# Closing stages of a two-layer graph attention by pairs of node tiles

## The chip, the cores and the metric

The kernel is one program on one core of a Trainium2 chip. The metric is the device time of a whole launch in microseconds (us), as the median of several runs.

## The reference, cut to what matters

12500 nodes of 256 features, padded to 98 tiles of 128 nodes; 200000 edges, sorted by destination. First comes a node network with a residual, then two layers of graph attention, four heads of 64 and one head of 256.

```python
x = x + L0_gnn(relu(layernorm(x)), ...)       # segment sums, MLP 608 -> 1024 -> 256
h = relu(layernorm(x))
def gat(h, W, a_src, a_dst, b, heads):
    h = (h @ W).reshape(n, heads, -1)
    al_s, al_d = sum(h * a_src), sum(h * a_dst)        # per node and head
    e = leaky_relu(al_s[src] + al_d[dst], 0.2)         # every node has an edge to itself, too
    m = segment_max(e, dst); ex = exp(e - m[dst])
    den = segment_sum(ex, dst)
    return segment_sum(h[src] * (ex / den[dst]), dst) + b
h = elu(gat(h, W1, ..., b1, heads=4))
x = x + gat(h, W2, ..., b2, heads=1)
```

## The kernel before, in words

The program runs stage after stage. A stage (`stage`, line 44) has its own buffers and semaphores and ends in a barrier of all engines, so that nothing of one stage runs beside another. Every engine has its own program within a stage and they meet in semaphores. `steps` (line 905 and after) writes the first and last turns of a loop out and puts the others into a hardware loop; `At` gives the index `n`, a buffer `slot` and a `par`ity.

1. `structure`, `masks` and `edge_chains`: tables of the edges, and sums and maxima along them. The change leaves these alone.
2. `node_mlp`: 49 steps, each with a pair of node tiles. TensorE multiplies; VectorE adds the first products (`add_first`, line 1564), makes features and statistics and turns PSUM into SBUF; ScalarE has ReLU and square roots; GpSimd gathers rows. The result `x1` of the node network goes to DRAM, and so does `table1`, which is the layer-normed `x1` times the weights of the first attention, with its scores of sources (`als`) behind it; the scores of destinations (`ald`) stay in SBUF. In a step TensorE waits for the hidden rows of this pair (`hid_ready`, line 1450) before it makes the table rows of the pair before (line 1456).
3. `clear`: GpSimd (line 1899) and VectorE (line 1904) write zeros to the accumulators `acc`, 98 tiles of 264 numbers per partition.
4. For each of the two layers: `open_layer` splits `ald` into three bf16 numbers (lines 1637 to 1641, VectorE alone), `attention` walks over 64 batches of 26 groups of edges, and `close_layer` makes rows of nodes of the sums.
5. `attention`: GpSimd gathers 26 times per batch (line 578) by the indices that SP has loaded (line 530); TensorE, ScalarE and VectorE make weights and add the products to `acc`. VectorE first clears `drow` (line 906), and SP's loads (lines 522 to 536) begin behind the wait for it (`blank`).
6. `close_layer` (lines 1651 to 1865) has a lead and a loop over 98 node tiles. In the lead the weights and the bias are loaded, VectorE projects the attention vectors of the second layer through its weights (first layer only, lines 1266 and 1267), and then works out the share of the sums, `ga`, and that of the node's own edge, `gb`, for all nodes (lines 1812 to 1828), with two exponentials on ScalarE. The loop, first layer, with what an engine does for one tile `n`:
   - SP loads the node's own row (`hrow`, four buffers, line 1705) and stores the table row of tile `n-2` (line 1719).
   - GpSimd: `own = hrow * gb` (line 1736), then `own + bias` (line 1741).
   - VectorE: `t1 = acc * ga` (line 1846), `y = t1 + own` (line 1849), `mn = min(y, 0)` (line 1852), and for tile `n-1` the last of the ELU, `h2 = exp(mn) - 1 + relu(y)` (line 1862).
   - ScalarE: ReLU, exponential, the zeros for `acc` of this tile (lines 1779 to 1781); then, for `n-2`, it copies the projection out of PSUM (`als`, `ald`, `grow`, lines 1789 and 1791); then, for `n-1`, the turned rows to SBUF (line 1795).
   - TensorE, for `n-1`: two transposes of `h2` (line 1756), a wait until ScalarE has copied them, then two multiplications by the second layer's weights (line 1763; each has two records in the trace).

   In the last layer there are no TensorE and ScalarE parts in the loop. `x1` is loaded too (`xrow`, line 1707), `t1 = acc * ga + xrow` is one instruction (line 1843), GpSimd and `y` are as above, and `y` is stored as the output (line 1715).

## Time and profile before

| | us |
|---|---|
| median of three runs | 6883.79 (6879.75 to 6888.57) |
| the profiled execution, its own time | 6892.58 |
| its span, first to last instruction | 6890.8 |
| TensorE busy | 4795.7 (70%) |
| VectorE busy | 4425.4 (64%) |
| GpSimd busy | 3704.5 (54%) |
| ScalarE busy | 3018.8 (44%) |
| mean granted TensorE clock | 0.836 of full |

No engine is busy all the time. As the stages follow one another behind barriers, the span is a sum of stages, and shares of the whole span say little: each stage is to be read by itself. The last column but one of a windows row is the granted clock: 1.00 is 2.4 GHz and 0.50 is 1.2 GHz.

### The profile page before, as it was taken

To read this page: it belongs to the slowest core of one execution; us is meant where nothing else is said; L and a number is where in the kernel's file an instruction comes from. 1 tells how busy PE (TensorE), PEld (TensorE's weight loads), DVE (VectorE), ACT (ScalarE), POOL (GpSimd) and SP (SyncE) were. 2 spreads that over 40 slices of the span, in tenths; PEclk is the share of its full clock that TensorE was granted. 3 is DMA by queue.
4 is the path that set the end of the run, shared out by engine and by line. 5 is a ranking of instruction groups with operands and counts; after the bars stand their busy time and mean duration, and the time that the engine had idled before them with its cause. 6 is when DMAs were issued, how large, how long until landed. Compare 5 with 4: busy or idle time off the path is not lost. (4 is left out here: it accounts for less than half of the span.)

```text
span 6890.8 us, 105434 instructions
## 1 busy us (share of the span) xinstructions
PE 4795.7 (70%) x22853; PEld 3495.8 (51%) x22853; DVE 4425.4 (64%) x12670; ACT 3018.8 (44%) x8326; POOL 3704.5 (54%) x4025
## 2 busy tenths in 40 slices
PE   0065666999995777777777776757777777777770
PEld 0044445777773555555555554535555555555540
DVE  7399996555554666666666666645555555555558
ACT  4044442222223666666666665534433443443330
POOL 5200000111106777777777774457777777777758
PEclk9988888999996888888888887558888888888885
DMA  1299996333323444444444443334444444444437
GB/s 37 85 371 396 402 400 231 105 104 104 105 96 91 119 119 121 120 119 119 121 119 120 121 119 75 83 87 109 110 109 109 110 109 110 109 110 110 109 85 220
DMA packets 382596, 964.82 MB, mean 140 GB/s; under 512 B 105887, under 2 KB 222982, under 8 KB 357399
## 3 DMA queue, kind: packets, MB, share of 16 engines
q0 software_dynamic: 168928, 459.50, 25.4%
q1 hardware_dynamic: 206504, 452.76, 19.2%
q10 hardware_dynamic: 7056, 51.38, 1.9%
q8 instruction: 35, 0.57, 0.0%
q14 instruction: 73, 0.60, 0.0%
HBM read 696.58 MB, written 266.77 MB: 140 GB/s over the span
## 5 line engine op out<-in xcount | busy, mean ns | idle before, releaser
L578 POOL DMA_INDIRECT rows<-table_d,idx x3328 | 3160.3, 950 | 1048.0 <-issue 899.4
L639 PE MATMUL pG<-rows,onehot 128*128 128x264 f32 (+1 forms) x6656 | 2175.9, 474 | 585.6 <-issue 343.8
L639 PEld LDWEIGHTS pG<-rows,onehot 128*128 128x128 f32 x6656 | 1487.4, 236 | 1119.9 <-issue 462.1
L866 DVE TENSOR_TENSOR acc<-acc,pG 128x264 f32 (+1 forms) x3328 | 1417.7, 426 | 966.9 <-PE pG L639 587.6
L730 ACT ACTIVATE rows<-rows 128x64 f32<-128x64 f32 (+1 forms) x4480 | 1249.9, 368 | 0.0
L723 ACT ACTIVATE onehotT<-pQ 128x1024 bf16<-128x1024 f32 (+1 forms) x512 | 442.4, 864 | 1317.8 <-PE pQ L611 1317.8
L712 ACT ACTIVATE onehot<-pQ 128x1024 f32<-128x1024 f32 (+1 forms) x512 | 441.1, 862 | 536.3 <-PE pQ L596 533.5
L1152 PE MATMUL pH<-hT_pre,w1h 128*128 128x256 f32 x1568 | 437.9, 436 | 212.3 <-ACT pre L1090 204.3
L1210 DVE SCALAR_TENSOR_TENSOR run<-run,same_e,ea 128x96 f32<-128x96 f32 x1567 | 490.1, 313 | 4.9 <-DMA ea<-in_ea 4.2
L1210 DVE SCALAR_TENSOR_TENSOR run<-run,cut_e,ea 128x96 f32<-128x96 f32 x1567 | 490.0, 313 | 0.1
L1152 PEld LDWEIGHTS pH<-hT_pre,w1h 128*128 128x128 f32 x1568 | 333.4, 221 | 297.3 <-ACT pre L1090 222.8
L848 DVE TENSOR_TENSOR rows<-rows,pA 128x1024 f32<-128x1024 f32 x384 | 466.8, 1216 | 4.4
L1393 POOL COPY idx_agg<-k_end 128x2 int32 (+1 forms) x49 | 9.0, 184 | 748.5 <-DVE feat L1554 745.5
L1121 POOL DMA_INDIRECT fix_e<-rows_d,head_i x1 | 1.0, 958 | 762.4 <-DMA rows_d<-run 762.4
L619 PE MATMUL pS<-adt,onehotT 128*128 x3328 | 389.6, 177 | 4.8 <-issue 4.2
L1460 PE MATMUL pM<-w,hid 128*128 128x256 f32 x1568 | 354.4, 379 | 1.1 <-ACT hid L1472 1.1
L611 PE MATMUL pQ<-drow,k_nrow 128*128 128x512 bf16 (+1 forms) x896 | 318.8, 431 | 50.8 <-DMA drow<-drow_d 41.2
L1424 PE MATMUL pM<-fT,w1e 128*128 128x256 f32 x1568 | 352.5, 383 | 0.0
L619 PEld LDWEIGHTS pS<-adt,onehotT 128*128 128x128 bf16 x3328 | 298.7, 97 | 91.9 <-issue 5.7
L596 PE MATMUL pQ<-k_nrow,drow 128*128 128x128 bf16 x3328 | 301.6, 235 | 35.6 <-ACT onehotT L723 33.0
L1424 PEld LDWEIGHTS pM<-fT,w1e 128*128 128x128 f32 x1568 | 294.6, 190 | 54.8 <-issue 16.6
L1460 PEld LDWEIGHTS pM<-w,hid 128*128 128x128 f32 x1568 | 297.8, 190 | 43.1 <-ACT hid L1472 1.3
(302 smaller groups left out, 5416.7 us busy)
## 6 DMA issues: line engine op xcount, KB each, us to landing
rows_d<-run SPq DMA_DIRECT2D x98, 1536.0 KB, 11.2
ea<-in_ea SPq DMA_DIRECT2D x98, 768.0 KB, 13.8
rows<-table_d,idx POOLq DMA_INDIRECT x3328
pre_d<-pre ACTq DMA_DIRECT2D x49, 1024.0 KB
pre_in<-pre_d SPq DMA_DIRECT2D x49, 1024.0 KB, 5.9
tab<-tab_d SPq DMA_DIRECT2D x64, 392.0 KB
hrow_cl<-table_d SPq DMA_DIRECT2D x196, 128.0 KB, 2.5
table_d<-g_rows SPq DMA_DIRECT2D x49, 260.0 KB
```

Source lines behind the costliest of these rows:

```text
L578: g.indirect_dma_start(out=rows[:, at.par, k, 0:XF + H], out_offset=None, in_=table, in_offset=bass.IndirectOffsetOnAxis(ap=idx[:, at.par, ...
L619: mm = pe.matmul(pAD[:, k, :, :].rearrange("p m h -> p (m h)"), onehotT[:, k, :], adt[:, bass.ds(tiles[k], 1), :, :].rearrange("p o m h -> ...
L639: mm = pe.matmul(pG[(k + 2 * at.par) % 4][:, 0:W], onehot[:, k, :], rows[:, at.par, k, :], start=True, stop=True)
L712: a.activation(onehot[:, ks[0]:ks[-1] + 1, :].rearrange("p k e -> p (k e)"), pQ[:, 0:len(ks), :].rearrange("p k e -> p (k e)"), ACT.Relu). ...
L723: a.activation(onehotT[:, ks[0]:ks[-1] + 1, :].rearrange("p k e -> p (k e)"), pQ[:, 0:len(ks), :].rearrange("p k e -> p (k e)"), ACT.Relu) ...
L730: ins = a.activation(part, part, ACT.Copy, scale=rows[:, at.par, k, XF + h:XF + h + 1])
L848: v.tensor_tensor(part, part, by, ALU.mult).then_inc(weighed_dve, 1)
L866: v.tensor_tensor(to, to, pG[(k + 2 * at.par) % 4][:, 0:W], ALU.add).then_inc(added, 1)
L1152: mm = pe.matmul(pH[k % 4][:, 0:N2], w1h[:, i, k * P:(k + 1) * P], hT[:, n % 2, i, :], start=(i == 0), stop=(i == 1))
L1210: v.scalar_tensor_tensor(out=run[:, g % BUFS, k, m, :], in0=before, scalar=by[:, e:e + 1], in1=ea[:, g % BUFS, k, :], op0=op0, op1=op1).th ...
L1424: mm = pe.matmul(pM1[kk][:, h * N2:(h + 1) * N2], w1e[:, i, cols], fT[:, at.par, i, :], start=False, stop=(i == 1), skip_group_check=True)
L1460: mm = pe.matmul(pM2[:, t * XF:(t + 1) * XF], hid[:, at.par, k, t * P:(t + 1) * P], w2[:, k, :], start=(k == 0), stop=(k == HC - 1), skip_ ...
```

## The change

**Node stage.** TensorE's waits for `hid_ready` and `x1_ready` move behind the table rows of the pair's first tile. `x1` goes to DRAM with the second layer's bias already added, from buffers of its own (`x1b`, one VectorE addition of 128x512 per pair, placed after the copies of the table rows), and in an order of rows in which the two rows of a partition are neighbours. Four more loads are issued ahead of the first layer's weights. The second layer's attention vectors are projected here, in step 0, and the widened weights `wg2` are stored to DRAM at the end.

**Opening.** The stages `clear` and `open_layer` are gone. Their work is done by VectorE at the start of `attention`, for each layer: clear `drow`, then the five instructions of the split, then zeros for all of `acc` (128x25872). SP issues the loads of indices and tables before it waits for `blank`.

**First closing.** 49 steps with a pair of tiles each. The order is another: the rows `y` are turned by TensorE before the ELU, ScalarE adds the bias as it copies them from PSUM (then it is one number per partition), and minimum, exponential and `max(exp - 1, w)` are made on turned rows. So TensorE turns pair `n-1` and multiplies pair `n-2` in one step, and does not wait for a copy in between. The addition of the bias on GpSimd, ReLU, the clearing and the copy `h2T` on ScalarE fall away.

**Last closing.** 49 steps, VectorE alone, four instructions per pair, each 128x256. GpSimd has no part, and six pairs are loaded ahead instead of four tiles.

```diff
 # attention: sync
-            sp.wait_ge(blank, 1)
             load_idx(one)
-            load_drow(one)
+            load_idx(two)
             load_jpe(one)
-            load_idx(two)
             load_tab(one)
             load_jv(one)
+            sp.wait_ge(blank, 1)
+            load_drow(one)
             load_drow(two)
...
 # attention: tensor
+            pe.wait_ge(opened, 5)
             destinations(one, node_tiles_of(one), first=True)
...
 # attention: vector
+            v.memset(drow[:, :, :, :], 0.0).then_inc(blank, 1)
             v.memset(R[:, :, :], -BIG).then_inc(vec, 1)
             v.memset(arow[:, :, :], -BIG).then_inc(vec, 1)
-            v.memset(drow[:, :, :, :], 0.0).then_inc(blank, 1)
+            chain = Chain(v, opened)
+            ald = keep["ald"][:, :, 0:H]
+            rest = onehot[:, 0:H, 0:NT].rearrange("p h j -> p j h")
+            chain(v.tensor_copy(adt[:, :, 0, :], ald))
+            chain(v.tensor_tensor(rest, ald, adt[:, :, 0, :], ALU.subtract))
+            chain(v.tensor_copy(adt[:, :, 1, :], rest))
+            chain(v.tensor_tensor(rest, rest, adt[:, :, 1, :], ALU.subtract))
+            chain(v.tensor_copy(adt[:, :, 2, :], rest))
+            chain(v.memset(acc[:, :, :], 0.0))
...
 # node_mlp
+            sp.dma_start(g2b[:, :], io["g2_b"]...).then_inc(late_in, 16)
+            sp.dma_start(wg2[:, :, 0:XF], io["g2_w"]...).then_inc(late_in, 16)
+            for m, name in enumerate(("g2_src", "g2_dst")):
+                sp.dma_start(att2[:, m, :], io[name]...).then_inc(late_in, 16)
...
-                    sp.wait_ge(x1_ready, prev.n + 2)
-                    sp.dma_start(tile2(x1v, prev.n), x1[:, prev.par, :, :]).then_inc(x1_out[prev.par], 16)
+                    sp.wait_ge(x1b_ready, prev.n + 1)
+                    sp.dma_start(tile2(x1v, prev.n), x1b[:, prev.par, :, :]).then_inc(x1_out[prev.par], 16)
...
+            sp.wait_ge(wg2_ready, 1)
+            sp.dma_start(dr["wg2"], wg2[:, :, :]).then_inc(late_in, 16)
...
-                if mlp:
-                    pe.wait_ge(hid_ready, at.n * KK + KK)
-                    pe.wait_ge(x1_ready, at.n + 1)
                 for t in range(2):
...
                         mm.then_inc(go_ready, 1)
                     if mlp:
+                        if t == 0:
+                            pe.wait_ge(hid_ready, at.n * KK + KK)
+                            pe.wait_ge(x1_ready, at.n + 1)
                         for k in range(HC):
...
+                if back:
+                    biased(prev, None if n is None else n - 1)
                 if front:
                     residual(nxt)
+                if n == 0:
+                    v.wait_ge(late_in, 16 * 4)
+                    project_attention(v, chain, wg2, att2, tmp, 1)
+                    v.sem_inc(wg2_ready, 1)
...
 # close_first: gpsimd
+                g.tensor_tensor(own[:, at.par, :, :]..., hrow[:, at.slot, :, :]...,
+                                two(gb, at.n)....to_broadcast([P, 2 * H, D]), ALU.mult).then_inc(own_ready, 1)
...
 # close_first: tensor
+                    prev = at.plus(-1)
+                    pe.wait_ge(y_ready, prev.n + 1)
+                    pe.wait_ge(w_ready, prev.n - 1)
+                    for i in range(2):
+                        for u in range(2):
+                            mm = pe.transpose(pT[prev.par]..., y[:, prev.par, u, i * P:(i + 1) * P], keep["ident"][:, :])
+                    mm.then_inc(t_ready, 1)
...
+                    prev = at.plus(-2)
+                    pe.wait_ge(h2_ready, prev.n + 1)
+                    pe.wait_ge(o_copied, prev.n - 1)
+                    for u in range(2):
+                        for i in range(2):
+                            mm = pe.matmul(pO[prev.par][:, u, 0:WG], h2T[:, prev.par, i, u * P:(u + 1) * P], wg[:, i, :],
...
 # close_first: scalar
+                    for i in range(2):
+                        ins = a.activation(w[:, prev.par, i, :], pT[prev.par]..., ACT.Identity, bias=bias[:, i:i + 1])
+                    ins.then_inc(w_ready, 1)
+                    a.wait_ge(mn_ready, prev.n + 1)
+                    a.activation(ex[:, :, :], mn[:, :, :], ACT.Exp).then_inc(ex_ready, 1)
...
+                    a.activation(two(keep["als"], prev.n)[:, :, 0:1], pO[prev.par][:, :, XF:XF + 1], ACT.Copy)
+                    a.activation(two(keep["ald"], prev.n)[:, :, 0:1], pO[prev.par][:, :, XF + 1:XF + 2], ACT.Copy)
+                    a.activation(grow[:, prev.slot, :, :], pO[prev.par][:, :, 0:XF + 1], ACT.Copy).then_inc(o_copied, 1)
...
 # close_first: vector, the order of one step
+                if now:
+                    scaled(at, n)            # t1 = acc * ga
+                if back:
+                    lowered(prev)            # mn = min(w, 0)
+                if now:
+                    joined(at)               # y = t1 + own
+                if back:
+                    elu(prev, ...)           # h2T = max(ex - 1, w)
...
 # close_last: vector
+                for u in range(2):
+                    v.scalar_tensor_tensor(out=t1[:, at.par, u, :], in0=tile(acc, u)[:, 0:XF], scalar=tile(ga, u),
+                                           in1=xrow[:, at.slot, u, :], op0=ALU.mult, op1=ALU.add).then_inc(summed, 1)
...
+                    v.scalar_tensor_tensor(out=y[:, at.slot, u, :], in0=hrow[:, at.slot, u, :], scalar=tile(gb, u),
+                                           in1=t1[:, at.par, u, :], op0=ALU.mult, op1=ALU.add).then_inc(y_ready, 1)
```

## Rows read from the trace of the kernel before

**Rows 1.** Windows by stage: length, busy us (instructions) of PE, PEld, DVE, ACT, POOL; clock; DMA.

```profile
1135.00:2088.00 953.00, 905.48 (x4780) 753.77 (x4780) 548.77 (x1747) 233.40 (x487) 97.13 (x138) 0.99 0.32 101
...
2150.00:4246.00 2096.00, 1574.94 (x7775) 1108.20 (x7775) 1312.76 (x3390) 1331.77 (x4349) 1553.87 (x1637) 0.84 0.45 118
4246.00:4575.00 329.00, 235.05 (x588) 152.98 (x588) 230.71 (x414) 171.62 (x688) 141.95 (x197) 0.54 0.37 80
```

**Rows 2.** Timeline of the first closing in its middle, TensorE: start, duration in us.

```profile
4401.26 2.09 PE L1763 MATMUL pO_cl<-wg_cl,h2T_cl 128*128 128x258 f32 x4 [0.58 <-ACT h2T_cl L1795]
...
4403.14 0.63 PE L1756 MATMUL pT_cl<-k_ident,h_cl 128*128 128x128 f32 x2
...
4404.52 2.08 PE L1763 MATMUL pO_cl<-wg_cl,h2T_cl 128*128 128x258 f32 x4 [0.75 <-ACT h2T_cl L1795]
```

**Rows 3.** The same near its beginning, where the granted clock is full.

```profile
4280.68 1.14 PE L1763 MATMUL pO_cl<-wg_cl,h2T_cl 128*128 128x258 f32 x4 [0.66 <-ACT h2T_cl L1795]
...
4281.66 0.38 PE L1756 MATMUL pT_cl<-k_ident,h_cl 128*128 128x128 f32 x2
...
4282.69 1.14 PE L1763 MATMUL pO_cl<-wg_cl,h2T_cl 128*128 128x258 f32 x4 [0.66 <-ACT h2T_cl L1795]
```

**Rows 4.** Timeline of the last closing, one tile of its steady part.

```profile
6744.13 0.94 DVE L1843 SCALAR_TENSOR_TENSOR t_cl<-acc,ga_cl,xrow_cl 128x256 f32<-128x256 f32 x1
...
6745.10 0.72 DVE L1849 TENSOR_TENSOR y_cl<-t_cl,own_cl 128x256 f32<-128x256 f32 x1
```

**Rows 5.** DMA queue of SP from 6725 to 6888: packets, MB, share of 16 engines.

```profile
q1 hardware_dynamic: 41040, 37.37, 76.1%
```

**Rows 6.** Timeline: lead and end of the first closing, then the lead of the last.

```profile
4246.18 0.37 SPq L1697 DMA_DIRECT2D bias_cl<-in_g_b  x1
...
4255.46 0.57 DVE L1812 TENSOR_TENSOR es_cl<-k_als,k_ald 128x392 f32<-128x392 f32 x1
...
4265.90 0.43 DVE L1846 TENSOR_TENSOR t_cl<-acc,ga_cl 128x256 f32<-128x256 f32 x1
...
4571.34 0.39 ACT L1791 ACTIVATE grow_cl<-pO_cl 128x257 f32<-128x257 f32 x1
...
6713.83 0.35 SPq L1697 DMA_DIRECT2D bias_cl<-in_g_b  x1
...
6717.31 0.33 DVE L1812 TENSOR_TENSOR es_cl<-k_als,k_ald 128x98 f32<-128x98 f32 x1 [4.64 <-DMA bias_cl<-in_g_b]
...
6722.43 0.93 DVE L1843 SCALAR_TENSOR_TENSOR t_cl<-acc,ga_cl,xrow_cl 128x256 f32<-128x256 f32 x1 [0.16 <-DVE gb_cl L1828]
```

**Rows 7.** Timeline of the openings: clearing, first loads and first scores; then the second layer's.

```profile
2091.54 10.88 POOL L1899 MEMSET acc<- 128x12936 f32 x1 [80.52 <-ACTq L52]
2094.30 10.84 DVE L1904 MEMSET acc<- 128x12936 f32 x1 [6.28 <-issue]
...
2113.18 0.36 SPq L530 DMA_DIRECT2D idx<-src_d  x1
...
2149.42 0.27 DVE L789 TENSOR_TENSOR ad<-rows,ad 128x104 f32<-128x104 f32 x1 [20.21 <-DMA rows<-table_d,idx]
...
4574.91 0.25 DVE L1637 CAST adt<-k_ald 128x98 bf16<-128x98 f32 x1 [7.88 <-PEq L55]
...
4580.97 0.34 SPq L530 DMA_DIRECT2D idx<-src_d  x1
```

**Rows 8.** Groups of instructions by line: busy us, mean ns; idle time before them and its releasers.

```profile
L1090 ACT ACTIVATE pre<-pH,b_in 128x256 f32<-128x256 f32 x392 | 167.6, 466 | 81.0 <-PE pH L1152 79.1
L1472 ACT ACTIVATE hid<-hid 128x512 f32<-128x512 f32 x196 | 122.8, 626 | 136.2 <-DVE hid L1564 136.1
L1456 PE MATMUL pGo<-wg,h1T 128*128 128x264 f32 x392 | 110.1, 404 | 17.9 <-ACT hid L1472 15.4 <-DVE h1T L1598 1.8 <-DVE g_rows L1613 0.7
L1540 DVE TENSOR_TENSOR x_rows<-res,pM 128x512 f32<-128x512 f32 x49 | 33.7, 688 | 77.7 <-PE pM L1460 77.7
```

**Rows 9.** Timeline of the node stage, the first result of its VectorE.

```profile
1152.00 0.69 DVE L1540 TENSOR_TENSOR x_rows<-res,pM 128x512 f32<-128x512 f32 x1 [5.97 <-PE pM L1460]
```

More of the change, by code:

```diff
@@ L1698, in _ @@
[L1698 to L1702 removed]
+            sp.dma_start(bias[:, :], io["g1_b"].rearrange("(k p) -> p k", p=P), allow_slow_non_contiguous=True).then_inc(b_in, 16)
@@ L1805, in _ @@
             chain = Chain(v, vec)
-            cnt = keep["cnt"]
-            als, ald = keep["als"][:, :, 0:H], keep["ald"][:, :, 0:H]
-            v.wait_ge(w_in, 16 if last else 64)
-            if not last:
-                project_attention(v, chain, wg, att, t1[:, 0, :], 1)
-            chain(v.tensor_tensor(es[:, :, :], als, ald, ALU.add))
-            chain(v.scalar_tensor_tensor(out=es[:, :, :], in0=es[:, :, :], scalar=0.2, in1=es[:, :, :],
-                                         op0=ALU.mult, op1=ALU.max))
```

370 lines of the change are left out of this document (187 added, 183 removed).

## The prediction

> **What bounds the kernel now.** I read the busy time by windows first, cut at the barriers [rows 1]. Four stretches matter. In the node stage TensorE is busy 905.5 of 953 us at a granted clock of 0.99: it is the bound, and only its idle 47 us can be had. In an attention stage GpSimd issues a gather about every 2096/1637 = 1.28 us from end to end; the change touches nothing in that loop, so both attention loops keep their length and can only start earlier. The first closing takes 329 us and nobody is busy all of it: TensorE 235, VectorE 231, at a granted clock of 0.54. The last closing runs from 6713.8 to the end of the span at 6890.8, 177 us [rows 6].
>
> The timeline says why the first closing is slow [rows 2]. TensorE multiplies for 2.09 us, has its transposes (0.63 us) just behind, and then stands still until ScalarE has copied the turned rows; the next multiplication starts 3.26 us after the one before. In between ScalarE must, by its program order, copy the last product out and only then the turned rows. It is a ring: product, copies, turned rows, product. The reader should also see the level of the clock: the four records take 2.09 us here and 1.14 us in rows 3, which is 1.2 against 2.4 GHz. With the full clock a round took 4282.69 - 4280.68 = 2.01 us, and there TensorE was busy (1.14 + 0.38)/2.01 = 76% of it. It then fell to the half clock and stayed there, busy (2.09 + 0.63)/3.26 = 83% of a round, until the last turns.
>
> In the last closing VectorE and GpSimd, which has two instructions per tile beside VectorE's two, hold each other up [rows 4]. The scaling takes 0.94 us and the addition 0.72, where the same shape takes 0.43 us when GpSimd is quiet (the instruction at 4265.90 [rows 6]). So two GpSimd instructions cost VectorE 0.51 + 0.29 = 0.8 us per tile. The DMA engines aren't far behind: 76.1% busy with that queue alone [rows 5].
>
> **First closing, lead.** From the first load at 4246.18 to the first softmax instruction at 4255.46 are 9.3 us, of loading and projecting [rows 6]. Both leave; the rest up to 4265.90 (10.4 us) stays. Gain 9.3.
>
> **First closing, loop.** Cost of one pair, engine by engine.
> - TensorE at full clock: four products 2 x 1.14 and four transposes 2 x 0.38 = 3.0 us; at the half clock 2 x 2.09 + 2 x 0.63 = 5.4 us [rows 2, 3].
> - VectorE: three instructions of 128x512 with two inputs at 0.69 (the row of line 1540 [rows 8]) and one minimum, at most 0.69, by my reading 0.45 as it has one input: 2.5 us. GpSimd keeps one instruction of 512 elements instead of two of 256 twice; I charge VectorE for it what two instructions cost in rows 4, 0.8 us. That makes 3.3. Bounds: 2.5 if it falls into VectorE's waits, 4.1 if the two hold each other up throughout, as 2 x 0.8.
> - ScalarE: two copies with bias at 0.466 [rows 8], one exponential 0.63, one copy of 514 columns, also 0.63, two tiny ones: 2.4 us. Not the bound.
> - The ring that held the loop before is gone, since turned rows are a step old when they are multiplied. What is late next is a longer ring over two steps: product 2.3, copies out 0.8, bias copies 0.9, minimum 0.45, exponential 0.63, last of the ELU 0.69, together 5.8 us with no hand-over counted, so 2.9 per pair, or 3.9 at the half clock. It is just under VectorE. SP issues two DMAs per pair; the loads are four pairs ahead.
>
> At full clock VectorE is therefore the bound, at 3.3; I take 3.6 us, since hand-overs (minimum to exponential to ELU, 0.63 against the 0.69 of the addition put between) won't all be hidden. With TensorE at half clock it would be 5.4. Which clock? At 5.4 TensorE would have no pause at all, and work without pause is what holds 0.99 in the node stage [rows 1]; at 3.6 it is busy 3.0/3.6 = 83%, more than the 76% of rows 3, from which it fell after some rounds. So it may fall, but then it has no pauses and comes back. I take mostly the full clock. The end: 49 x 3.6 = 176 plus a drain of 9 us through ScalarE, TensorE and ScalarE again. From the first scaling to the last copy it was 4571.7 - 4265.9 = 305.8 us [rows 6], it will be 185. Gain 121, so with the lead 130.
>
> The Trainium skill's page "TensorE: Matmul & The Clock Gate", section "HAM oscillation — how this bites in real kernels", speaks against this part: pauses between groups of products make the clock swing between its levels even without long gaps. By that rule the loop would spend part of its time at 5.4, and the rival below has the price.
>
> **Last closing.** The wait for the bias, 6717.31 - 6713.83 = 3.5 us [rows 6], leaves. In the loop VectorE has four instructions with two SBUF inputs per pair at about 0.48 (between 0.43 and the 0.6 of a per-partition scalar I allow), 1.9 us, and nobody to share with. DMA: the queue was busy 76.1% of 163 us, in which some 95 tiles passed, so 1.31 us per tile, 2.6 per pair of the same bytes; `x1` comes in half as many descriptors, which can save nothing or up to a sixth. I take 2.5 (2.3 to 2.9) per pair: the DMA engines become the bound. 49 x 2.5 = 123, with 4 us for the first and last landing 127, against 177. Gain 50. SP was issuing three DMAs per tile and now issues three per pair.
>
> **Openings.** First layer: SP's first load of indices moves from 2113.18 to the start of the stage after the node stage, which is where GpSimd's clearing began, 2091.54 [rows 7]. Gain 21.6. VectorE now has `drow`, the split, and 25872 columns of zeros, 2 x 10.84 = 21.7 us, in all some 27 us, and up to 30 if it starts as late as at 2094.30. The cover is the first batch's gathers: from SP's first load to the first scores 2149.42 - 2113.18 = 36.2 us, so it is free; without the cover each us over 36 would cost one. TensorE's new wait is for the split only, which stands ahead of the zeros. Second layer: the stage of the split began at 4574.91, and the loads at 4580.97; now they begin where it did. Gain 6. The zeros are again under the gathers, and off ScalarE in the closing.
>
> Does a long memset hold up gathers, which GpSimd issues? No row shows that pair. The nearest is GpSimd's own memset beside VectorE's: 10.88 and 10.84 us for equal work, so neither stood still [rows 7]. Bounds: nothing, or the whole 21.7 per layer. I take nothing.
>
> **Node stage.** TensorE's pause before line 1456, put down to the hidden rows, sums to 15.4 us in 49 steps [rows 8]; the table rows of the first tile now run inside it: gain 14 (0 to 15). The bias addition, 0.69 per pair, stands before the residual, whose end is followed by 77.7/49 = 1.6 us of waiting for products [rows 8]: hidden with 0.9 us to spare; without that cover it costs 34 us in all. The projection in step 0 (some 3.7 us) meets a pause of 5.97 [rows 9]. Four loads ahead of the weights delay the start by their issues, 4 x 0.5 = 2 us. At the end the addition, the later store of `x1` and the store of `wg2` add 1.5. Net gain 10.5.
>
> **Sum.** 130 + 50 + 21.6 + 6 + 10.5 = 218 us. The profiled execution took 6892.58, so 6674.6; the median lies 8.8 below it: 6666 us.
>
> **The rivals.**
> 1. *The clock stays at its half level in the first closing.* For it: before, the half clock lasted for almost the whole stage at 83% busy. Against: that loop had a pause in every round, this one would have none. Price: 49 x (5.4 - 3.6) = 88 us, 6754. Chance 0.14.
> 2. *The zeros hold up the gathers.* VectorE's memset of 21.7 us stands beside the first gathers of each layer; if descriptors can't be written meanwhile, the opening gains almost nothing: + 2 x 21.7 = 43 us, 6709. For it: VectorE is held up beside GpSimd in rows 4. Against: the two memsets of rows 7. Chance 0.10. The Trainium skill's "SBUF — State Buffer", section "Who interferes with whom", gives that trap for two-port modes alone and frees an instruction with at most one SBUF input; by the first reading it would be 6709, by the second 6666.
> 3. *The stages of a pair don't overlap, and it is slower than before.* Place: the first closing. If a pair had to pass all engines before the next one (addition 0.69, transposes 1.26, bias copies 0.93, minimum 0.45, exponential 0.63, ELU 0.69, products 4.18, copies 0.97 = 9.8 us at half clock), 49 x (9.8 - 3.6) = 304 us more, 6970. It decides from 3.6 + 218/49 = 8.0 us per pair. Against it: two buffers of everything but `mn` and `ex`, and an order that takes pair n-2 behind n-1. Chance 0.03.
> 4. *The change does less than it says*: the pause in the node stage is not filled and the bias addition is exposed, 14 + 34 = 48 us, 6714. Chance 0.05.
>
> **How the numbers follow.** The forecast, a pair between 3.0 and 4.2 us in the first closing and 2.3 to 2.9 in the last, has 0.68. Its own range: low by 0.6 x 49 + 0.2 x 49 = 39, high by 29 + 20 = 49, so 6627 to 6715, which takes in rivals 2 and 4. The range reaches to rival 1: 6627 to 6754. About 0.2% is what a measurement can tell from no change; only rival 3 comes near or past that: faster 0.96, same 0.01, slower 0.03.
>
> **What would show it right or wrong.** In the first closing: products of successive pairs start 3.6 us apart, eight records in 2.3 us, a granted clock above 0.9, VectorE busy over 90%. Products 5.4 apart with no idle TensorE would be rival 1. In the last closing: DMA share above 0.9 and VectorE idle behind `xrow` or `hrow`. At the openings: gathers begin 2 us behind the first load and go on every 1.25 us beside the memset; a hole of 20 us would be rival 2. In the node stage: no pause before line 1456 and still one before the result. The forecast is wrong if the first closing isn't shortened by at least 80 us.

## The result, and the profile after

The changed kernel takes 6613.67 us (median of 4 runs, 6610.30 to 6614.39) against 6884.64 us of the kernel before on the same chip: a ratio of 0.961, 95% interval 0.959 to 0.962. It is 271 us faster. The forecast was 6666 us (6627 to 6754): the direction is right, the size is not, and the time lies 13 us below the low end. The span of the profiled execution is 6612.3 us, 278.5 less than that of the profile before; the stages below are added up against these two spans. They differ by 7.5 us more than the medians do.

Windows of the changed kernel: the node stage, the first attention loop, the beginning and the body of the first closing, the second attention loop, the body of the last closing (columns as in [rows 1]; the last three numbers are the granted clock, the DMA share and GB/s, so the clock is the last but two, not the last but one as stated above the prediction):

```profile
1123.00:2069.00 946.00, 897.97 (x4802) 755.53 (x4802) 591.57 (x1833) 234.76 (x490) 98.96 (x141) 0.98 0.31 105
2071.00:4199.00 2128.00, 1561.91 (x7744) 1102.38 (x7808) 1338.85 (x3400) 1334.91 (x4353) 1576.14 (x1664) 0.84 0.44 118
4211.00:4225.00 14.00, 8.33 (x29) 6.47 (x29) 10.01 (x13) 5.16 (x15) 7.04 (x5) 0.57 0.30 77
4225.00:4360.00 135.00, 112.69 (x509) 78.44 (x510) 129.87 (x170) 88.79 (x256) 62.65 (x43) 1.00 0.59 164
4379.00:6506.00 2127.00, 1551.85 (x7744) 1088.12 (x7808) 1245.75 (x3400) 838.97 (x1664) 1574.63 (x1664) 0.83 0.40 108
6515.00:6600.00 85.00, 0.00 (x0) 0.00 (x0) 72.20 (x176) 0.00 (x0) 0.00 (x0) 0.50 1.08 388
```

Two rows are new in kind. In the body of the first closing VectorE is busy 129.87 of 135 us and TensorE has its full clock; before, it had 0.54 of it over the stage [rows 1]. In the last closing the DMA share is 1.08 at 388 GB/s. The share adds up the time of every packet, so 1.08 means that packets of one engine overlapped.

Cut at the first work of each stage, the spans (us) compare so; the four rows on closings and openings carry nine tenths of it:

| stage | before | after | gain | forecast |
|---|---|---|---|---|
| all before the node stage | 1108.3 | 1106.3 | 2.0 | 0 |
| node stage | 983.3 | 962.9 | 20.4 | 10.5 |
| clearing and first opening | 21.6 | 0 | 21.6 | 21.6 |
| first attention loop | 2133.0 | 2131.5 | 1.5 | 0 |
| first closing | 328.7 | 177.8 | 150.9 | 130 |
| second opening | 6.1 | 0 | 6.1 | 6 |
| second attention loop | 2132.9 | 2129.7 | 3.2 | 0 |
| last closing | 177.0 | 104.2 | 72.7 | 50 |

**The first closing**, one pair's VectorE and GpSimd, one product of TensorE and the next pair's scaling, from the timeline of the changed kernel (start, duration, engine; in brackets the idle time before and what ended it); rows 2 and 3 held its counterpart:

```profile
4225.01 0.69 DVE L1854 SCALAR_TENSOR_TENSOR h2T_c<-ex_c,w_c 128x512 f32<-128x512 f32 x1
4225.06 1.54 POOL L1760 TENSOR_TENSOR own_c<-hrow_c,gb_c 128x512 f32<-128x512 f32 x1 [2.73 <-DVE y_c L1844]
...
4225.62 1.53 DVE L1837 TENSOR_TENSOR t_c<-acc,ga_c 128x512 f32<-128x512 f32 x1
...
4225.76 2.01 PE L1788 MATMUL pO_c<-wg_c,h2T_c 128*128 128x258 f32 x8
...
4227.08 0.41 DVE L1848 TENSOR_SCALAR mn_c<-w_c 128x512 f32<-128x512 f32 x1
4227.41 0.68 DVE L1844 TENSOR_TENSOR y_c<-t_c,own_c 128x512 f32<-128x512 f32 x1
...
4228.79 1.53 DVE L1837 TENSOR_TENSOR t_c<-acc,ga_c 128x512 f32<-128x512 f32 x1
```

VectorE has no idle time in brackets at all: a pair is 4228.79 - 4225.62 = 3.17 us, and it is ELU, scaling, minimum and addition end to end. Over all 49 pairs, from 4211.1 to 4366.1, it is 3.23 us. The scaling takes 1.53 us, although its first instance took 0.69 for the same shape (it and GpSimd's first multiplication both stand at 4211.10, and the scaling went first): some 0.85 us are not its own.

**The last closing**, late in its body:

```profile
6596.65 0.88 DVE L1934 SCALAR_TENSOR_TENSOR t_c<-acc,ga_c,xrow_c 128x256 f32<-128x256 f32 x2 [0.36 <-DMA xrow_c<-x_d]
...
6597.45 0.88 DVE L1940 SCALAR_TENSOR_TENSOR y_c<-hrow_c,gb_c,t_c 128x256 f32<-128x256 f32 x2
...
6598.69 0.88 DVE L1934 SCALAR_TENSOR_TENSOR t_c<-acc,ga_c,xrow_c 128x256 f32<-128x256 f32 x2 [0.37 <-DMA xrow_c<-x_d]
```

and its DMA queue from 6515 to 6606 (packets, MB, share), beside [rows 5]:

```profile
q1 hardware_dynamic: 30800, 35.32, 107.6%
```

A pair takes 2.04 us, of which VectorE waits 0.37 for the rows of `x1`.

**The opening**, beside [rows 7]: indices, the first gather, VectorE's zeros, a gather beside them and the first scores.

```profile
2069.14 0.83 SPq L531 DMA_DIRECT2D idx<-src_d  x2
...
2071.07 0.94 POOL L579 DMA_INDIRECT rows<-table_d,idx  x1 [83.46 <-DMA idx<-src_d]
...
2080.28 0.95 POOL L579 DMA_INDIRECT rows<-table_d,idx  x1 [0.30 <-issue]
...
2081.44 21.62 DVE L917 MEMSET acc<- 128x25872 f32 x1 [5.46 <-issue]
2081.53 0.95 POOL L579 DMA_INDIRECT rows<-table_d,idx  x1 [0.30 <-issue]
...
2105.77 0.27 DVE L791 TENSOR_TENSOR ad<-rows,ad 128x104 f32<-128x104 f32 x1 [1.87 <-DMA rows<-table_d,idx]
```

Gathers are 1.25 us apart (2081.53 - 2080.28) before and beside the memset alike, and the scores come 36.6 us after the indices, as before (36.2).

### The profile page after: what moved, and what is told of

Same layout as the page of the kernel before. It is cut to its first block and busy times, and to the rows that moved or that the text cites. A ratio compares the mean times of both kernels' runs of the same rounds, so it can differ in the third digit from the quotient of the medians.

```text
span 6612.3 us, 102298 instructions
## 1 busy us (share of the span) xinstructions
PE 4628.9 (70%) x22725; PEld 3413.7 (52%) x22853; DVE 4352.8 (66%) x12524; ACT 2950.7 (45%) x7934; POOL 3469.3 (52%) x3679
## 5 line engine op out<-in xcount | busy, mean ns | idle before, releaser
L640 PEld LDWEIGHTS pG<-rows,onehot 128*128 128x128 f32 x6656 | 1471.2, 233 | 1127.0 <-issue 455.1
L1484 PE MATMUL pM<-w,hid 128*128 128x256 f32 x1568 | 354.4, 379 | 0.9 <-ACT hid L1496 0.9
L1448 PEld LDWEIGHTS pM<-fT,w1e 128*128 128x128 f32 x1568 | 295.3, 191 | 55.1 <-issue 16.6
L612 PE MATMUL pQ<-drow,k_nrow 128*128 128x512 bf16 (+1 forms) x768 | 274.6, 414 | 59.2 <-DMA drow<-drow_d 29.9
```

The lines of the kernel that those rows point to most:

```text
L640: mm = pe.matmul(pG[(k + 2 * at.par) % 4][:, 0:W], onehot[:, k, :], rows[:, at.par, k, :], start=True, stop=True)
L1448: mm = pe.matmul(pM1[kk][:, h * N2:(h + 1) * N2], w1e[:, i, cols], fT[:, at.par, i, :], start=False, stop=(i == 1), skip_group_check=True)
L1484: mm = pe.matmul(pM2[:, t * XF:(t + 1) * XF], hid[:, at.par, k, t * P:(t + 1) * P], w2[:, k, :], start=(k == 0), stop=(k == HC - 1), skip_ ...
```

## The experiments

Fourteen runs follow, of twelve kernels and twice the changed one again, on four chips. On three of them the attention loops took 2650 to 2790 us instead of 2131 (gathered rows land later), and the kernel before was slower there too, so whole times of different groups can't be compared. From the node stage on, every stage that a run left alone kept its length to 2 us from chip to chip (the part ahead of it ended between 1106.3 and 1113.2), so the effects are read from the length of the stage. The unchanged first closing took 177.2 to 177.5 us in these runs, the unchanged last one 103.6 to 104.9.

### The order of the first closing

The kernel before, with the product one step later (ScalarE's copies out follow at tile n-3):

```diff
                 mm.then_inc(t_ready, 1)
-                pe.wait_ge(t_copied, prev.n + 1)
-                if n is None or n >= 3:
+                if n is not None and not 2 <= n <= NT + 1:
+                    return
+                prev = at.plus(-2)
+                pe.wait_ge(t_copied, prev.n + 1)
+                if n is None or n >= 4:
                     pe.wait_ge(o_copied, prev.n - 1)
```

> The kernel before, with one thing of the change alone: in the first closing TensorE turns tile n-1 and then multiplies tile n-2 (a step later), ScalarE copies the product of tile n-3 out. Tiles, GpSimd's two instructions and the zeros stay. Theory (the ring of product, copies out and turned rows set the 3.26 us of a tile, not the work): the ring is then spread over two tiles, TensorE's own 2.09 + 0.63 = 2.7 us at the half clock or VectorE's 2.4 become the bound: 2.7 to 2.8 us per tile at the half clock, some 45 us less than before (6840), and up to 60 less if the clock comes back. Rival (only pairs, the turned ELU and one GpSimd instruction made the closing short): 3.1 us or more per tile, at most 15 us less (6870).

Measured: closing and second opening together (up to the next load of indices) take 261.3 us instead of 334.8, so 73.5 less, 2.33 us per tile; the ratio to before is 0.991 (0.990 to 0.993). The clock came back too. Window of its body:

```profile
4880.00:5080.00 200.00, 128.06 (x520) 84.95 (x518) 193.89 (x345) 147.89 (x605) 138.19 (x173) 0.91 0.54 113
```

Some 45 us were expected, up to 60 with the clock back; it was more. The order alone is worth half of the 150.9 us. The lead is worth 9.2; how the rest divides among pairs, the turned ELU, the zeros and GpSimd's second instruction, no run separates. What bounds then is VectorE (193.89 of 200), with scaling and addition at 0.83 us each beside GpSimd's two instructions, where the same shape takes 0.43 alone [rows 6].

The opposite, in the changed kernel: the product back in the step of its pair.

```diff
-                if n is None or n >= 2:
-                    prev = at.plus(-2)
+                if n is None or 1 <= n <= NS:
                     pe.wait_ge(h2_ready, prev.n + 1)
-                    if n is None or n >= 4:
+                    if n is None or n >= 3:
                         pe.wait_ge(o_copied, prev.n - 1)
```

> The changed kernel with the product of the first closing back in the step of its pair: TensorE turns pair n-1 and then waits for the ELU of pair n-1. Theory (the two-step pipeline is what makes pairs pay): turn 0.66, two copies with bias 0.93, minimum 0.41, exponential 0.63, ELU 0.69 and product 2.0 stand in one chain: 5.4 us with hand-overs 5.6 per pair at the full clock, 49 x 2.4 = 118 us more than the changed kernel (about 6730); TensorE is then busy 48% of a pair, and if its clock falls for it, a pair takes 8.1 us and the time is about 6850. Rival (VectorE is the bound whatever the order): below 4.0 us per pair, at most 40 us more (6655).

Measured: 6.72 us per pair; the closing takes 354.4 us, 177 more than changed (177.8) and 26 more than the closing of before (328.7). The window of its body:

```profile
4850.00:5120.00 270.00, 159.69 (x479) 121.21 (x477) 123.65 (x157) 81.57 (x236) 57.38 (x39) 0.75 0.26 75
```

and, from the timeline:

```profile
4903.92 3.60 PE L1787 MATMUL pO_c<-wg_c,h2T_c 128*128 128x258 f32 x8 [2.78 <-DVE h2T_c L1853]
...
4907.35 0.60 PE L1778 MATMUL pT_c<-k_ident,y_c 128*128 128x128 f32 x4
```

It lies between the two figures expected, because the clock does: after a pause of 2.8 us the eight products take 3.6 us, where they take 2.01 at 2.4 GHz, and the transposes behind them are at full speed again (0.60 us). Without the later step this stage would have been slower than before, so the pairs pay only with it; the step pays without the pairs, 73.5 us.

### What a pair waits for

`ex` of the first closing in PSUM instead of SBUF:

```diff
-        ex = sb("ex", [P, 2, N2])
+        ex = c.enter_context(nc.psum_tensor("ex_c1", [P, 2, N2], F32))
```

> The changed kernel with the exponential of the first closing kept in PSUM instead of SBUF, nothing else. Theory (the 0.85 us by which VectorE's scaling of 128x512 is longer than 0.68 is waiting for GpSimd's multiplication, which could not start before the ELU ended, since both read two SBUF inputs): the ELU then has one SBUF input, GpSimd's multiplication runs beside it, the scaling falls from 1.53 to about 1.0 us and a pair from 3.17 to 2.7 us, where TensorE (0.66 + 2.01) is the next bound: about 20 us less than the changed kernel (6593). Rival (the scaling is slow for its own operands or for the port of the sums, and GpSimd's work beside it is a coincidence): the scaling stays at 1.5 and a pair at 3.2 us, no change (6614).

Measured: 2.87 us per pair, the closing 159.8 us instead of 177.8. The durations of the scaling (min/median/max in ns, 49 instances), changed kernel first:

```profile
L1837 DVE TENSOR_TENSOR t_c<-acc,ga_c x49: 677/1530/1533, 4211.1 to 4366.1; 128x512 f32 x36, 128x512 f32<-128x512 f32 x13
```

```profile
L1837 DVE TENSOR_TENSOR t_c<-acc,ga_c x49: 678/1080/1387, 4803.2 to 4940.8; 128x512 f32 x36, 128x512 f32<-128x512 f32 x13
```

Nothing in the scaling was touched, yet its median fell by 0.45 us. GpSimd's multiplication starts at the ELU in both kernels, but its record is 1.54 us long in the changed one and 1.04 here:

```profile
4881.36 0.69 DVE L1854 SCALAR_TENSOR_TENSOR h2T_c<-ex_c,w_c 128x512 f32<-128x512 f32 x1
4881.49 1.04 POOL L1760 TENSOR_TENSOR own_c<-hrow_c,gb_c 128x512 f32<-128x512 f32 x1 [1.68 <-DVE y_c L1844]
```

It no longer stands still until the ELU has ended, and is out of the scaling's way 0.5 us sooner.

GpSimd's multiplication left out (SP's loads then wait for VectorE):

```diff
-                v.wait_ge(own_ready, at.n + 1)
-                v.tensor_tensor(y[...], t1[...], own[:, at.par, :, :], ALU.add)
+                v.wait_ge(own_in[at.slot], at.half * 16 + 16)
+                v.tensor_tensor(y[...], t1[...], hrow[:, at.slot, :, :], ALU.add)
```

> The changed kernel with GpSimd's multiplication of the node's own rows left out of the first closing; VectorE adds the loaded rows unscaled. It leaves the own share gb out of the computation. Theory (GpSimd's instruction costs VectorE 0.85 us): scaling 0.68, minimum 0.41, addition 0.68, ELU 0.69 are 2.46 us, and TensorE's 2.67 us are the bound: 2.7 to 2.75 us per pair, 49 x 0.45 = 22 us less than the changed kernel (6592). Rival (hand-overs between the engines set the 3.17 us): a pair stays above 3.0 us, less than 8 us gained (6606).

Measured: 2.82 us per pair, 157.7 us, with the scaling at 0.68 to 0.69 us in all 49 pairs:

```profile
L1836 DVE TENSOR_TENSOR t_c<-acc,ga_c x49: 681/684/693, 4806.4 to 4941.9; 128x512 f32 x36, 128x512 f32<-128x512 f32 x13
```

The price of GpSimd is 20 us of closing, and hand-overs do not set 3.17. But this kernel stops 0.15 us above TensorE's 2.67 and the one before it 0.2, which neither theory said.

Is it two SBUF inputs that exclude? Two kernels with `ex` and the scaled sums `t1` in PSUM (`t1` then has one buffer instead of two), GpSimd released at different points; first behind the scaling:

```diff
+                if n is None or n >= 1:
+                    g.wait_ge(summed, at.n)
```

> The changed kernel with the exponential and the scaled sums of the first closing in PSUM, and GpSimd's multiplication released by the end of VectorE's scaling instead of by its addition. Theory (GpSimd's and VectorE's instructions exclude each other only where both read two SBUF inputs): of VectorE's four instructions only the scaling still reads two; the multiplication (1.04 us) fits beside the minimum and the addition (0.41 + 0.69), the scaling comes down to 0.68 and a pair to 2.7 us, the work of TensorE; the first closing takes 154 us instead of 177.8 and the 159.8 of the run with the exponential alone in PSUM. Rival (the exclusion holds for every pair of instructions and only the start of the multiplication matters): the addition grows to 1.1 us or more and a pair takes 2.85 us or more.

Measured: 3.35 us per pair, 183.2 us, worse than the changed kernel. The addition did not grow (0.68), as the theory has it, but the minimum did, to 1.22 us (median), for it has one SBUF input and was held off all the same:

```profile
4881.33 1.04 POOL L1762 TENSOR_TENSOR own_c<-hrow_c,gb_c 128x512 f32<-128x512 f32 x1 [2.44 <-DVE t_c L1839]
4881.40 1.26 DVE L1850 TENSOR_SCALAR mn_c<-w_c 128x512 f32<-128x512 f32 x1 [0.25 <-ACT w_c L1810]
4882.58 0.68 DVE L1846 TENSOR_TENSOR y_c<-t_c,own_c 128x512 f32<-128x512 f32 x1
```

So the theory was incomplete. A minimum of 512 columns in 0.41 us, where a two-input instruction takes 0.69, looks like a faster mode. The Trainium skill, "SBUF — State Buffer", section "Who interferes with whom", says that `tensor_scalar` can enter a mode which takes both ports and then excludes GpSimd; these two rows agree. That it is the mode, and nothing else about this instruction, no run separates; that the minimum excludes GpSimd's multiplication is shown.

The second one is released behind the minimum:

```diff
+                    g.wait_ge(mn_ready, at.n - 1)
                     g.wait_ge(y_ready, at.n - 1)
```

> As in the run before (exponential and scaled sums of the first closing in PSUM), but GpSimd's multiplication is released by the end of VectorE's minimum. Theory (of VectorE's four instructions two exclude GpSimd: the scaling, with two SBUF inputs, and the minimum, which with one SBUF input takes 0.41 us for 512 columns where the others take 0.69, so it uses both ports; addition and ELU, with one input in PSUM, do not): the multiplication (1.04 us) runs wholly beside addition and ELU (0.69 + 0.69), all four are at their own lengths, 2.47 us, and TensorE's 0.66 + 2.01 set 2.7 us per pair: the first closing takes 153 to 155 us (159.8 with the exponential alone in PSUM, 177.5 changed, 183.2 with the other release). Rival (every VectorE instruction excludes GpSimd's): the addition or the ELU grows by 0.3 us or more, a pair takes 3.2 us or more.

Measured: all four instructions at their own length, GpSimd's too:

```profile
L1838 DVE TENSOR_TENSOR t_c<-acc,ga_c x49: 687/690/723, 4860.0 to 4997.2; 128x512 f32 x36, 128x512 f32<-128x512 f32 x13
...
L1849 DVE TENSOR_SCALAR mn_c<-w_c x49: 426/427/428, 4864.6 to 5000.9; 128x512 f32<-128x512 f32 x49
L1855 DVE SCALAR_TENSOR_TENSOR h2T_c<-ex_c,w_c x49: 690/692/692, 4865.7 to 5002.0; 128x512 f32<-128x512 f32 x49
```

The exclusion is settled, instruction by instruction. The time is not what was expected: 2.86 us per pair and 159.7 us, no better than with `ex` alone in PSUM. VectorE has idle time (busy 66.81 of 80 us), and something else sets the pace. The next kernel tests a cycle over two pairs, in ScalarE's order (`scores` holds the two small copies that leave their old place):

```diff
                     ins.then_inc(w_ready, 1)
+                if n is None or n >= 3:
+                    scores(at.plus(-3))
...
-                    a.activation(two(keep["als"], prev.n)[:, :, 0:1], ...)
-                    a.activation(two(keep["ald"], prev.n)[:, :, 0:1], ...)
                     a.activation(grow[:, prev.slot, :, :], ...)
```

> The last kernel with the exponential and the scaled sums in PSUM and GpSimd's multiplication behind the minimum, and one thing more: ScalarE's two small copies of the attention terms (0.17 us each) move from behind the exponential to between the bias copies and the exponential, where ScalarE waits 0.49 us for the minimum, and belong to the pair before. Theory (a cycle over two pairs sets 2.86 us: product, three copies out 0.9 to 1.1, bias copies 0.84, minimum 0.43, exponential 0.60, ELU 0.69, product 2.01, with hand-overs 5.7 us): the cycle is 0.3 us shorter, 2.7 us per pair, the first closing takes 152 us instead of 159.7. Rival (TensorE with 93% busy time is the bound already and its own gaps make the 2.86): no change, 159 to 160 us.

> The changed kernel again, as the base for the kernel beside it: first closing 177.5 us; the other kernel's whole time should lie some 25 us below it by the theory, 18 by the rival.

Measured side by side: 2.75 us per pair on average, later 2.69 (TensorE's transposes at 4282.64 and 4285.33), the closing 154.3 us against 177.4, the whole 6588.65 us against 6611.10 (against before 0.958, 0.957 to 0.959, and 0.961, 0.960 to 0.963). It beats both kernels, the changed one by 22 us. Two successive pairs of TensorE and the start of ScalarE's bias copies:

```profile
4282.64 0.66 PE L1780 MATMUL pT_c<-k_ident,y_c 128*128 128x128 f32 x4
...
4283.38 0.83 ACT L1817 ACTIVATE w_c<-pT_c,bias_c 128x256 f32<-128x256 f32 x2
...
4283.48 2.01 PE L1791 MATMUL pO_c<-wg_c,h2T_c 128*128 128x258 f32 x8 [0.19 <-DVE h2T_c L1866]
...
4285.33 0.65 PE L1780 MATMUL pT_c<-k_ident,y_c 128*128 128x128 f32 x4
```

TensorE now has no pause but 0.19 us: it is the bound. Moving 0.34 us of small copies gave 0.11 us per pair on average, 5.4 us in all, so the rival falls: the cycle was the bound, by a little. The closing is 2 us longer than the 152 expected.

### Node stage

The two waits put back ahead of the products of the table rows (line 1477):

```diff
+                if mlp:
+                    pe.wait_ge(hid_ready, at.n * KK + KK)
+                    pe.wait_ge(x1_ready, at.n + 1)
                 for t in range(2):
...
-                        if t == 0:
-                            pe.wait_ge(hid_ready, at.n * KK + KK)
-                            pe.wait_ge(x1_ready, at.n + 1)
```

> The changed kernel with the node stage's two waits (hidden rows, result) put back ahead of the products of the table rows. Theory (a wait ahead of a group of products costs more than the idle time in the profile, as the start of the group can't overlap the end of the transposes before it): the node stage grows by 0.6 us per step, 49 x 0.64 = 31 us, from 962.8 to 994. Rival (the recorded idle time is the cost, as the prediction had it): + 14 us, 977.

> The changed kernel itself, as the base for the others on the same chip. In the first four runs the attention stages took some 2660 to 2720 us instead of 2131, while all other stages kept their lengths to 0.5 us. Expected here too: node stage 962.8 us, first closing 177.8, last closing 104.2.

Measured: the node stage takes 989.6 us against 961.4 of its base in the same group (first closings 177.4 and 177.2): 28.2 us for the waits. From the transposes to the products, changed kernel and then waits restored:

```profile
1500.50 0.44 PE L1471 MATMUL pG_<-k_ident,feat 128*128 128x128 f32 x2 [0.51 <-DVE h1T L1627]
1500.78 1.06 PE L1477 MATMUL pGo<-wg,h1T 128*128 128x264 f32 x4
```

```profile
1513.00 0.44 PE L1471 MATMUL pG_<-k_ident,feat 128*128 128x128 f32 x2 [0.51 <-DVE h1T L1627]
1513.83 1.15 PE L1480 MATMUL pGo<-wg,h1T 128*128 128x264 f32 x4 [0.39 <-ACT hid L1496]
```

The pause is recorded as 0.39 us, but the products start 0.83 us after the transposes instead of 0.28. The record counts from the end of the transposes; without a wait the next group starts before that end. Each such pause costs 0.58 us (28.2/49), not 0.39 or less.

### Last closing

The loads of `xrow` left out:

```diff
-                sp.dma_start(xrow[:, at.slot, :, :], of_pair(xv, at.n)).then_inc(own_in[at.slot], 16)
...
-                                           in1=xrow[:, at.slot, u, :], op0=ALU.mult, op1=ALU.add)
+                                           in1=hrow[:, at.slot, u, :], op0=ALU.mult, op1=ALU.add)
```

> The changed kernel with the loads of x1 left out of the last closing; the loaded table rows stand in their place in the sum, so the residual is left out of the computation. Theory (the DMA engines set the pace of 1.96 us per pair, VectorE needs 1.66): a third of the bytes less, VectorE becomes the bound: 1.66 per pair, 49 x 0.3 = 15 us less, the last closing takes 89 us instead of 104.2. Rival (VectorE or a wait of SP per pair sets the pace): 1.9 us or more per pair, at most 3 us less.

Measured: 86.1 us instead of 103.6, 1.59 us per pair; VectorE has no idle time left (72.00 of 72). The window, and the DMA queue in it:

```profile
7618.00:7690.00 72.00, 0.00 (x0) 0.00 (x0) 72.00 (x182) 0.00 (x0) 0.00 (x0) 0.50 0.99 322
...
q1 hardware_dynamic: 24036, 23.17, 98.8%
```

The DMA engines were the bound, with VectorE 0.4 us per pair behind. Their share is 0.99 here too, although VectorE now is the bound: the share alone doesn't tell which of the two it is.

GpSimd back, by pairs:

```diff
+                g.tensor_tensor(own[:, at.par, :, :], hrow[:, at.slot, :, :], gb[...], ALU.mult)
-                for u in range(2):
-                    v.scalar_tensor_tensor(out=y[...], in0=hrow[...], scalar=tile(gb, u), in1=t1[...], ...)
+                v.tensor_tensor(y[:, at.slot, :, :], t1[:, at.par, :, :], own[:, at.par, :, :], ALU.add)
```

> The changed kernel with GpSimd back in the last closing: it multiplies the pair's table rows by their share, VectorE adds them in one instruction of 512 columns; pairs, six buffers and the layout of x1 stay. Theory (GpSimd and VectorE exclude each other there, all instructions having two SBUF inputs): VectorE has 0.88 + 0.69 us and waits for GpSimd's 1.04, together 2.6 us per pair instead of the DMA engines' 2.0: the last closing takes 104 + 49 x 0.6 = 133 us. Rival (pairs and deeper buffers alone brought the gain, GpSimd fits into VectorE's 0.35 us of waiting and what is hidden): 2.1 us or less per pair, 108 us at most.

Measured: 124.9 us, 21 more than with VectorE alone (103.8); 2.36 us per pair. The two scalings take 1.65 us instead of 0.88 when GpSimd's 1.05 falls between them:

```profile
7862.58 1.65 DVE L1950 SCALAR_TENSOR_TENSOR t_c<-acc,ga_c,xrow_c 128x256 f32<-128x256 f32 x2
7862.90 1.05 POOL L1924 TENSOR_TENSOR own_c<-hrow_c,gb_c 128x512 f32<-128x512 f32 x1 [1.34 <-DVE y_c L1956]
```

The price is the exclusion's, though less than the 29 us expected. It is also less than a third of the 72.7 us gained in this stage: what GpSimd's leaving doesn't explain, some 50 us, belongs to the lead (3.6 us) and to pairs, six buffers instead of four and the bias addition, which no run separates.

`x1` in the old layout, in both stages:

```diff
-.rearrange("(s p t) f -> s p t f", p=P, t=2)
+.rearrange("(s t p) f -> s p t f", p=P, t=2)
```

> The changed kernel with x1 laid out as before (tile by tile) in the node stage and the last closing, so that its loads are of 1024 bytes per packet instead of 2048. Theory (a packet of 2048 bytes takes 86 ns on an engine and one of 1024 takes 47): 8 ns per row pair, 128 x 8 / 16 = 64 ns per pair of tiles, the last closing grows by 3 us, to 107. Rival (packet size doesn't matter, the bytes do): no change, 104; or (each packet has a cost of its own that counts fully): 2.6 us per pair, 135.

Measured: 105.8 us against 103.8, at 383 GB/s in its body instead of 390. Its DMA queue over 90 us:

```profile
q1 hardware_dynamic: 35579, 34.30, 108.9%
```

Packets of 1024 bytes instead of 2048 cost 2 us, near the 3 expected; the time alone is only 0.9 us above the longest unchanged last closing (104.9), but the lower rate bears it out.

### The cover of the zeros

```diff
             chain(v.memset(acc[:, :, :], 0.0))
+            chain(v.memset(acc[:, :, :], 0.0))
```

> The changed kernel with the zeros of the sums written twice by VectorE at the start of each attention stage. Cover theory (the zeros cost nothing until they end later than the first gathers land): the second memset ends 43.3 us after the first one began, 33.8 + 21.6 us after the first load of indices in the first layer, so the first scores stand 56.3 us after that load (56.9 - 1.6 in the second layer); on the chip of the profile shown they stood 36.6 us after it, which would be 19.7 us more per layer; on chips where they stood 54.0 us after it, 2 us more. Rival (the memset holds up gathers, which then land later by a part of it): the gathers' spacing beside the second memset is above 1.25 us, and the first scores come later than 57 us.

The zeros were written twice on a chip with late rows: the first scores stood 61.8 us after the indices (2136.4 - 2074.6) against 59.9 in the kernel beside it, so 1.9 us more; in the second layer 59.8 against 55.1, 4.7 more. The spacing of the gathers beside the second memset stayed 1.25 us (2113.14, 2114.39, 2115.63), so the rival falls; that twice the zeros cost so little there is shown. That one memset more would cost about 20 us with rows as early as in the profile shown was not seen. The sum missed one thing, the 5.46 us of "issue" that the second memset brings with it, which make 61.8 of the expected 56.3:

```profile
2086.84 21.62 DVE L917 MEMSET acc<- 128x25872 f32 x1 [5.46 <-issue]
2113.92 21.62 DVE L918 MEMSET acc<- 128x25872 f32 x1 [5.46 <-issue]
2135.90 0.48 DVE L784 TENSOR_REDUCE ad<-pS 128x104 f32<-128x312 f32 x1 [0.36 <-DVE acc L918]
```

## Why the prediction was right and wrong

**First closing, lead**: right. From the first load to the first scaling 10.5 us, against 19.7; forecast gain 9.3, measured 9.2.

**First closing, loop**: 142 us gained instead of 121. The step that failed here is "At full clock VectorE is therefore the bound, at 3.3; I take 3.6 us, since hand-overs ... won't all be hidden". The 3.3 was right: 3.17 in the steady part (0.69 + 1.53 + 0.41 + 0.68, less overlaps), with the charge of 0.8 for GpSimd at 0.85. The 0.3 for hand-overs was not there: VectorE waited 1.7 us for `ex` in the whole stage. The average of 3.23 against 3.6 is 18 us; the drain, 5 us instead of 9, is the rest. TensorE's 3.0 was 2.67 (0.66 + 2.01), which changed nothing. Why 0.8 was the charge is now shown, not only read off: VectorE and GpSimd exclude each other, by where the operands lie and by which instruction it is. The "longer ring over two steps", 5.8 us, was near: with the exclusion gone, a pair took 2.86 = 5.7/2, and shortening that cycle shortened the pair.

**Clock**: right as taken. It was granted half for the first pairs (0.57 over 14 us) and then full. Rival 1 (6754) falls. Its "this one would have none" does not hold, though: in the body TensorE is busy 112.69 of 135 us, the same 83% as in the loop before, and its transposes waited for `y` 43 times, 16.1 us in all. The granted clock was 1.00 all the same. The kernel with the product in its own step does swing (0.75), with a pause of 2.8 us before each product. What the prediction takes from the Trainium skill's "TensorE: Matmul & The Clock Gate" stands there in the section "A second HAM failure mode: psum-queue depth-cycling", not in the one that it names: in one other kernel TensorE idled briefly between groups of matmuls, often enough to make its clock oscillate. The trace of the kernel with the product in its own step agrees with that, the trace of the changed one, with its short pauses at 1.00, does not, and the measurement decides. What kept the loop of before at its half level at 83% busy, when the same work a step later had 0.91 at 64%, no run separates: it is open. That the forecast of a full clock came true is therefore in part luck.

**Last closing**: 72.7 gained instead of 50. The mechanism, "the DMA engines become the bound", is right; the term "I take 2.5 (2.3 to 2.9) per pair" is wrong: 1.95 over the stage, 2.04 late in it, 27 us less for 49 pairs (4 us of that were lost again, as the sum had left out the lead, 5.0 us from the first load to the first scaling). The step that failed is that it took the busy share as a linear measure of what is left, 76.1% busy for 2.6 us of work per pair. By [rows 5] the queue moved 37.37 MB / (0.761 x 163 us) = 301 GB/s per full share. When it was the bound it moved 35.32 / (1.076 x 91) = 361 per full share, and the share went past 1: 388 GB/s, 1.29 times as much, and 2.6 / 1.29 = 2.0. Larger packets are the smaller part of it: with `x1` in the old layout, all loads and stores in packets of 1024 bytes, it was 34.30 / (1.089 x 90) = 350 per full share, and with VectorE as the bound, same packets, 23.17 / (0.988 x 72) = 326. So the fuller the queue, the more a full share moved; why, no run shows (transfers are also twice as large as before, and the kernel without `x1` reads less). The next engine's work should have been the lower bound: with the prediction's own 1.9 for VectorE the low end would have been 6607, with the 1.6 that it took, 6593, and the measured time inside either way. This term is why the range missed.

**Openings**: right, 21.6 and 6.1. Rival 2, the zeros holding up gathers, falls: 1.25 us apart beside the memset, so none is seen. The Trainium skill's "SBUF — State Buffer", section "Who interferes with whom", frees a memset (no SBUF input) outside the two-port modes; the trace agrees. But the cover held by 1.9 us only in the first layer, where the prediction saw 6 to 9: the record of the memset began 5.5 us after the split ended.

**Node stage**: 20.4 instead of 10.5. "Gain 14 (0 to 15)" for the pause took 15.4 us of recorded idle time as the most there was; the pause is worth 28.2. Its costs were too low as well: from the stage's first load to the first `x_rows` it is 4.6 us longer than before (1154.6 - 1106.3 against 1152.0 - 1108.3), not 2, and from the last `x_rows` to the end 2.8 (17.6 against 14.8), not 1.5. The bias addition is hidden, as forecast: VectorE still waits for products after it, 43.2 us in 49 steps against the 77.7 of [rows 8]; the group of the changed kernel:

```profile
L1562 DVE TENSOR_TENSOR x_rows<-res,pM 128x512 f32<-128x512 f32 x49 | 33.7, 688 | 43.2 <-PE pM L1484 43.2
```

Rival 4 falls.

**Rival 3** (stages of a pair in series) was no outcome of this change, but the mechanism exists: 6.72 us per pair when the chain from transposes to product is put in series. Its price of 304 us was too high (measured 177): the clock then isn't at its half level throughout, and addition and copies out still run beside the chain.

Sum of the misses: 20.9 first closing, 22.7 last closing, 9.9 node stage, 2.0 ahead of it, 4.7 in the attention loops, that nobody touched, together 60 of 278.5 - 218. The last two, 6.7 us, are no more than what executions of one kernel differ by: the changed kernel's second attention loop took 2129.7 us here and 2124.8 in the last of the groups above, and its part ahead of the node stage 1106.3 to 1109.7.

## What to carry to other kernels

Where VectorE and GpSimd both have instructions with two SBUF inputs, look whether they exclude each other before you count them as two engines; here they did (1.53 us for 0.68), and so did the minimum of 0.41 us with its one. Moving one operand, `ex`, to PSUM bought 18 us; the second operand and the later release brought all instructions to their own length but no time, until the cycle behind them was shortened. A wait recorded as idle time on TensorE can be less than its price (0.39 us recorded, 0.58 paid), since the next group would have started under the end of the last. And a DMA share is no linear measure of what is left, nor does 0.99 prove a bound: work out bytes per time from a stretch where the queue is full, or leave the lower end at the next engine's work.

## What the hardware showed that was not expected

- A memset of 25872 columns holds VectorE for 27.08 us, not the 21.62 of its record: two in a row start 2113.92 - 2086.84 = 27.08 apart, and each record has 5.46 us of "issue" before it. The half-size one of [rows 7] began 2.76 us late in the same way. An opening can be 5.5 us shorter of cover than the record says.
- The length of a gather's issue was unchanged beside a memset (0.95 us), but grew to 1.14 and 1.16 us beside the split's subtraction and cast in the opening (2073.62 and 2075.07).
- The minimum of one SBUF input (0.41 us) waits for GpSimd's multiplication: 1.22 us when it starts behind it.
- Chips differ in how late gathered rows land: the first scores came 36.6 us after the load of indices, and 54.0 to 59.9 us after it on the others; attention loops took 2131 and 2650 to 2790 us, while the other stages from the node stage on were equal to 2 us.
